# Row transposes into the convolution's bank, both halves of the moments in one run with the transposes of h

## The reference

```python
    h = _L0_tok_ref(x, wte, w1, b1, w2, b2)        # tanh(shifted rows @ w1 + b1) @ w2 + b2
    h = h + _L0_attn_ref(_layernorm(h, axis=-1))   # rfft, |f|^2, top 6 lags, weighted sum
    h = h + _L0_ffn_ref(_layernorm(h, axis=-1), W, bias, A, Bf, coeffs, scales)
    # ffn: x W^T + bias + sum over 16 experts of low rank 16
```

## Time and profile before

| | |
|---|---|
| median of 3 runs | 415.15 us (414.15 to 416.32) |
| the profiled execution | 416.69 us |
| its span, first to last instruction | 414.8 us |
| matrix engine busy | 387.3 us, 93% |
| VectorE, ScalarE, GpSimd busy | 278.6, 246.2, 213.8 us |
| TensorE's granted clock, mean | 0.98 of full speed |
| HBM read, written | 12.40 MB, 67.12 MB |

### The profile page before, as it was taken

One profiled execution on the slowest core, in us unless ns is written; L12 is line 12 of the kernel. 1 busy time (PEld: TensorE's weight loads), 2 busy tenths in 40 slices (PEclk: granted clock), 3 DMA queues, 4 the chain that ended last, 5 costly groups with the idle time before them and its releaser, 6 DMA issues.

```text
span 414.8 us, 6528 instructions
## 1 busy us (share of the span) xinstructions
PE 387.3 (93%) x1908; PEld 280.9 (68%) x1908; DVE 278.6 (67%) x602; ACT 246.2 (59%) x362; POOL 213.8 (52%) x283
## 2 busy tenths in 40 slices
PE   1959987999999999999999999999999999999792
PEld 1535355777777777777777777777777777777461
DVE  3442443968686777777777868586968677776742
ACT  3033335767676767666757576666767676765641
POOL 6772430756647474747373747566555745222200
PEclk9978996999999999999999999999999999999998
DMA  8953010555454555555454555655546555555565
GB/s 191 370 200 111 0 22 2 205 196 232 149 230 174 210 219 212 218 212 212 174 219 164 220 200 205 221 205 182 233 147 233 185 208 218 202 202 202 205 280 230
DMA packets 27684, 79.86 MB, mean 193 GB/s; under 512 B 6186, under 2 KB 7482, under 8 KB 27668
## 3 DMA queue, kind: packets, MB, share of 16 engines
q1 hardware_dynamic: 23330, 75.45, 47.4%
q0 software_dynamic: 4096, 4.20, 4.7%
q10 hardware_dynamic: 242, 0.01, 0.0%
HBM read 12.40 MB, written 67.12 MB: 192 GB/s over the span
## 4 chain that ended last, share of the span: by engine, by line
PE 87%; DMA 3%; DVE 3%; SPq 2%; ACT 2%; issue 1%; ACTq 0%; DVEq 0%
PE o_ps L1057 45%; PE conv_ps L1148 14%; PE conv_ps L1154 7%; PE o_ps L1083 7%; DMA obuf<-in_scales 3%; PE o_ps L990 3%; PE sum_ps L1122 2%; PE mix_ps L1134 2%; PE sum_ps L1134 2%; PE et_ps L1112 2%; PE sum_ps L1096 1%; PE et_ps L1102 1%; SPq L313 1%; PE o_ps L1034 1%; DVE u_lo L868 1%
## 5 line engine op out<-in xcount | busy, mean ns | idle before, releaser
L405 POOL DMA_INDIRECT gathered<-in_wte,idx_now x128 | 128.2, 1002 | 44.2 <-issue 34.4
L509 ACT ACTIVATE obuf<-o_ps,mean_sb,a_sb 128x512 f32<-128x512 f32 x128 | 99.7, 779 | 80.4 <-PE o_ps L1083 53.0
L693 DVE TENSOR_SCALAR obuf<-o_ps,a_sb,mean_sb 128x512 f32<-128x512 f32 x128 | 102.3, 809 | 55.9 <-PE o_ps L1057 30.1
L1057 PE MATMUL o_ps<-w_hi,u_hi 128*128 128x512 f32 x256 | 111.1, 434 | 5.7 <-DVE u_lo L868 3.9
L1057 PE MATMUL o_ps<-w_hi,u_lo 128*128 128x512 f32 x256 | 101.6, 397 | 0.0
L1057 PE MATMUL o_ps<-w_lo,u_hi 128*128 128x512 f32 x256 | 101.6, 397 | 0.0
L1148 PE MATMUL conv_ps<-et_hl,shift_hi 128*128 128x512 f32 x256 | 66.6, 403 | 5.6 <-DVE et_hl L762 4.9
L1057 PEld LDWEIGHTS o_ps<-w_hi,u_hi 128*128 128x128 f32 x256 | 48.3, 189 | 28.2 <-issue 19.3
L1148 PEld LDWEIGHTS conv_ps<-et_hl,shift_hi 128*128 128x128 f32 x256 | 49.0, 193 | 18.5 <-issue 5.7
L433 POOL TENSOR_SCALAR var_eps<-var 128x8 f32<-128x8 f32 x16 | 3.5, 220 | 111.9 <-DVE var L820 111.9
L1057 PEld LDWEIGHTS o_ps<-w_lo,u_hi 128*128 128x128 f32 x256 | 48.3, 189 | 11.7
(11 more groups left out here) (133 smaller groups left out, 446.7 us busy)
## 6 DMA issues: line engine op xcount, KB each, us to landing
out<-obuf SPq DMA_DIRECT2D x63, 1024.0 KB, 4.0
h_all<-in_wT SPq DMA_DIRECT2D x4, 1024.0 KB, 12.6
gathered<-in_wte,idx_now POOLq DMA_INDIRECT x128
aT_sb<-in_aT SPq DMA_DIRECT2D x1, 1024.0 KB, 9.4
bfT_sb<-in_bfT SPq DMA_DIRECT2D x1, 1024.0 KB, 15.5
obuf<-in_w SPq DMA_DIRECT2D x2, 256.0 KB, 5.4
lagged<-xbar_twice SPq DMA_DIRECT2D x1, 512.0 KB, 3.7
out<-obuf SPq DMA_DIRECT2D x1, 512.0 KB, 3.9
```

The source lines that it names most:

```text
L405: pool.indirect_dma_start(gathered[p][:, i, :], None, wte, bass.IndirectOffsetOnAxis(ap=idx_now[p][:, i:i + 1].bitcast(U32), axis=0),).the ...
L509: nc.scalar.activation(obuf[:, q, i % 2, 0:512], o_ps[:, 2 * (i % 2), :], ACT.Identity, bias=mean_sb[pc][:, i:i + 1], scale=a_sb[pc][:, i: ...
L693: nc.vector.tensor_scalar(obuf[:, q, i % 2, 512:L], o_ps[:, 2 * (i % 2) + 1, :], a_sb[pc][:, i:i + 1], mean_sb[pc][:, i:i + 1], ALU.mult, ...
L1057: last = mm(o_ps[:, 2 * (i % 2) + n, :], lhsT, rhs[:, 512 * n:512 * (n + 1)], start=(i % 2 == 0 and f == 0), stop=(i % 2 == 1 and f == len ...
```

## The change

The row transposes write `conv_ps` in place of `et_ps`, and ScalarE (L519) and VectorE (L762) read them there. They now wait for `shifts_added` of the sequence before (the last reader of `conv_ps`), and in step 0 for `pad_conv_kept`, which `conv_half(0)` waited for until now. The second half of the moments is written to `et_ps` in place of `sum_ps` and stands directly behind the first half, ahead of the row transposes and odd tile 0; it waits for `xt_kept` of the sequence before in place of `h_ready`. `transpose_scaled` no longer waits for `et_lo_kept` ahead of the x transposes. No instruction with operands is added or removed.

```diff
@@ -192,7 +192,7 @@
         def y_view(hh):
-            return (mix_ps, sum_ps)[hh][:, 0:4 * (E + 3)].rearrange("p (j two n) -> p j two n", j=2, two=2)
+            return (mix_ps, et_ps)[hh][:, 0:4 * (E + 3)].rearrange("p (j two n) -> p j two n", j=2, two=2)
@@ -517,7 +517,7 @@
                         nc.scalar.copy(tiles_of(et_hl[u][0:E, PAD:SPAN], odd_tiles),
-                                       pair_bank(et_ps, odd_tiles)).then_inc(et_hi_kept, 1)
+                                       pair_bank(conv_ps, odd_tiles)).then_inc(et_hi_kept, 1)
@@ -759,7 +759,7 @@
-                        nc.vector.tensor_tensor(lo, pair_bank(et_ps, odd_tiles), hi.bitcast(F32), ALU.subtract).then_inc(et_lo_kept, 1)
+                        nc.vector.tensor_tensor(lo, pair_bank(conv_ps, odd_tiles), hi.bitcast(F32), ALU.subtract).then_inc(et_lo_kept, 1)
@@ -1097,7 +1097,6 @@
                     pe.wait_ge(x_ready, b + 1)
-                    ge(pe, et_lo_kept, 2 * (a + front))
                     for q in range(NT // 2):
@@ -1106,10 +1105,11 @@
                 def transpose_rows():
                     pe.wait_ge(rows_gathered[u], 16 * NT * (g + 1))
-                    ge(pe, et_lo_kept, 2 * a)
-                    ge(pe, xt_kept, a - 1)
+                    if in_step(0, g, u):
+                        pe.wait_ge(pad_conv_kept, 1)
+                    ge(pe, shifts_added, 2 * a)
                     for j in range(NT // 2):
-                        last = tr(et_ps[:, P * j:P * (j + 1)],
+                        last = tr(conv_ps[:, P * j:P * (j + 1)],
@@ -1127,8 +1127,8 @@
                     if hh == 1:
-                        pe.wait_ge(h_ready, b + 1)
-                    bank, width = (mix_ps, sum_ps)[hh], 2 * (E + 3)
+                        ge(pe, xt_kept, b)
+                    bank, width = (mix_ps, et_ps)[hh], 2 * (E + 3)
@@ -1139,7 +1139,6 @@
                     if in_step(0, g, u) and hh == 0:
                         pe.wait_ge(shift_set, 2)
                         pe.wait_ge(pads_set, 2)
-                        pe.wait_ge(pad_conv_kept, 1)
@@ -1187,12 +1186,11 @@
                 if mid:
                     transpose_h()
                     moments_of(0)
+                    moments_of(1)
                 if front:
                     transpose_rows()
                 if back:
                     odd_tile(0)
-                if mid:
-                    moments_of(1)
                 if back:
                     even_tile(1)
                     four_rank_terms(1)
```

## The result

| | before | after |
|---|---|---|
| median | 414.65 us (413.12 to 416.32, 4 runs) | 421.27 us (420.91 to 422.13, 4 runs) |
| ratio | | 1.0167, 95% interval 1.0132 to 1.0203 |
| the profiled execution | 416.69 us | 421.24 us |
| its span | 414.8 us | 419.3 us |
| matrix engine busy | 387.3 us, 93% | 388.4 us, 93% |

What follows compares the result with a forecast made beforehand. The matrix engine, carrying 87% of the chain that ended last, was taken to bound the kernel. Terms 0 + 5.2 + 1.6 = 6.8 us on the median 415.15 gave 422.0 us, range 419.5 to 424.5.

Steps and rivals of the forecast that it cites:

- the matrix engine's own work: Steps 2 to 16: the four moved fp32 records take 0.46 us in either place, so joining the groups gains 0.
- stall of the convolution, 14 steps: At the first half of the convolution, waiting for VectorE's L762: 0.37 us in each of 14 steps, 5.2 us.
- the first step: Row transposes wait for pad_conv_kept until 25.58, the convolution comes 1.98 us later or more; +1.6 us taken, clock open.
- the end: Step 16 has the move but no convolution, and was given 0.
- The step on which I decided: Odd tile and VectorE's unbroken chain to L762 move 0.46 us later; the convolution has 0.09 room and stalls 0.37.
- Rival (c): Convolution not held by VectorE, the 0.05 us being its load's start anyway; only the first step left, 416.7 us; chance 0.05.
- Rival (a): At the convolution, the weight load overtakes the long wait: stall 0.26 us, 3.6 in 14 steps, total 420.4; chance 0.05.
- the sum by the row: At the convolution, against the skill's rule: the load itself starts 0.05 us after VectorE's end, 14 times of 14.
- the cheap case: First step: the slow clock stretch moves with the idle time, 0.85 us is won back, and the term is +1.1.
- the case that costs the same: First step: the slow clock stretch costs the same as before, and the term is +2.0 us.
- (d): First main product behind each fp32 group: joining saves 0.09 us in 15 places, 1.3 us; total 413.3; chance 0.03.
- (e): Stall in each step, or the longer first-step one, brings another slow clock stretch, 2.5 us or more: 424.5 and above; chance 0.06.

Runs made afterwards that it cites:

- the wait covered: Changed kernel with ScalarE's padding copy early and VectorE's low parts (L762) ahead of the second half of the variance: 413.27 us against 414.13, ratio 0.9988.
- the half move: Kernel before, with only one of the two products of the moments' second half ahead of the row transposes: 418.55 us against 413.62, ratio 1.0084.
- the second profile of the changed kernel: The changed kernel itself, unaltered, measured once more against the kernel before: 420.76 us against 413.62, ratio 1.0160.
- the banks alone: Changed kernel with the moments' second half back behind the first odd tile, new banks kept: 416.10 us against 414.13, ratio 1.0054.
- three pairs of kernels: Joined kernels with waits covered, against unjoined: 413.27 against before's 414.13; 408.28 against 409.34 (bias copy late in both); 406.96 against 407.62 (small loads early in both).
- VectorE's order alone: Kernel before, with only VectorE's low parts put ahead of the second half of the variance: one execution, 418.08 us against 414.02.
- the first four experiments: Moments moved alone on the kernel before (419.68 us); on the changed kernel: moments moved back (416.10), padding copy early (419.03), that plus low parts early (413.27).
- the first experiment: Kernel before, with only the moments' second half moved up, into conv_ps, rows staying in et_ps: 419.68 us against 414.13, ratio 1.0146.

## Why the prediction was right, point by point

The forecast was 422.0 us in 419.5 to 424.5, made as 415.15 + 6.8. Measured are 421.27 us, and +6.6 against the median of before in the same comparison (+7.1 in the second). By its terms:

| term | forecast | measured |
|---|---|---|
| the matrix engine's own work | 0 | step with the wait covered 21.90 against 21.91 |
| stall of the convolution, 14 steps | 5.2 | 14 x 0.365 = 5.1; alone +5.6 by the medians, 4.4 to 7.7 by the ratio, +5.0 group by group (last section) |
| the first step | 1.6 (1.1 to 2.0) | 2.0 by the medians, 1.3 to 3.1 by the ratio |
| the end | 0 | -0.3 |
| sum | 6.8 | 6.8 by these terms; 6.6 and 7.1 by the medians |

**The stall.** The step on which I decided holds in all its parts. The odd tile ends 0.46 later against the even tile ahead of it (VectorE's idle time before it grows from 0.46 to 0.92), VectorE's chain moves with it, the load follows L762 by 0.05, and 0.09 of it is absorbed: half the delay gave a step of 22.05, which is 0.14 above 21.91. Rival (c), that the 0.05 was an accident, would have left the step at 21.91 in the half move and in the whole one. Rival (a), by which the weights are loaded ahead of the wait, falls at the same place: the load starts at 209.91, behind the wait, and is idle for 0.54 before it. The Trainium skill ("TensorE: Matmul & The Clock Gate", What happens when you issue a matmul) says that weight loads are pulled ahead of matmuls in flight. Here the wait stands ahead of both the load and its matmul, and the load was not pulled ahead of it in any of the 14 steps; the sum by the row was right.

**The first step.** The wait was named rightly, and the price of the move as well: the transposes start at 25.58, as worked out. The uncertain part was the clock. In the profile after, the slow stretch is 21.98 to 28.81 instead of 26.37 to 33.20:

```profile
21.98:28.81 6.83, 3.23 (x10) 2.29 (x11) 1.43 (x3) 3.14 (x5) 2.91 (x5) 0.50 0.59 207
```

Only 3.2 us of work lie in it, where it was 5.6. So in this execution the stretch moved with the idle time, as in the cheap case, and the delay at the convolution of step 1 is 0.9 (54.89 against 53.95). In the second profile of the changed kernel the stretch is 2.2 us later, and the same convolution starts at 55.94, 2.0 behind before, as in the case that costs the same.

One step further on this delay is gone from both profiles. In step 1 the matrix engine stands still for 3.0 us, in the kernel before too, and the slow stretch behind that differs in length from execution to execution (stretches of the kernel before and after, then the step-2 convolution of each):

```profile
63.92:70.74 6.82, 6.04 (x22) 4.60 (x23) 1.71 (x4) 2.27 (x4) 0.00 (x0) 0.50 0.01 2
...
66.35:69.77 3.42, 3.42 (x14) 2.16 (x14) 0.81 (x1) 0.80 (x2) 0.00 (x0) 0.50 0.00 0
...
76.11 2.02 PE L1148 MATMUL conv_ps<-et_hl,shift_hi 128*128 128x512 f32 x8
...
76.09 2.13 PE L1147 MATMUL conv_ps<-et_hl,shift_hi 128*128 128x512 f32 x8
```

The second profile of the changed kernel has no slow stretch there, and its step-2 convolution starts at 75.65. So the two profiled executions differ by 4.55 us (421.24 against 416.69), near 5.1 for the loop's stalls less 0.3 at the end: the first step adds nothing to it. The prediction had named 423.5 us for the profiled execution. The first step's price rests on the times alone, 2.0 by the median of the banks alone (by the mean too), with an interval from 1.3 to 3.1. The working knew nothing of the second stretch, which alone moves a run by more than this whole term. That the forecast's 1.6 comes so near the measured 2.0, and the sum with it so near 6.8, is therefore in part luck; what it priced rightly is the delay as far as step 1, 0.9 and 2.0 in the two profiles against 1.1 and 2.0 in its two cases.

**What the sum missed.** The end gets shorter by 0.3 us. From the slot of the step-15 convolution to the end are 53.7 us before and with the banks alone, and 53.4 in every kernel with the whole move. In step 16 of the kernel before, VectorE's last step of u_lo meets GpSimd's copy of h (VectorE and GpSimd, kernel before):

```profile
386.24 1.00 DVE L845 TENSOR_TENSOR u_lo<-hT 64x512 fp32r<-64x512 f32 x1
...
385.97 0.73 POOL L449 COPY h_all<-u_rows 128x512 f32<-128x512 f32 x1
```

and after:

```profile
391.09 0.69 DVE L845 TENSOR_TENSOR u_lo<-hT 64x512 fp32r<-64x512 f32 x1
...
391.30 0.95 POOL L449 COPY h_all<-u_rows 128x512 f32<-128x512 f32 x1
```

With the variance later, VectorE's instruction comes first and runs at its usual 0.69; the matrix engine's wait behind it falls from 1.88 to 1.56. The two go together in all eleven profiles that have no slow stretch there: 1.00 and 53.7 in the four without the move, 0.69 and 53.4 in the seven with it. No run changes this order by itself.

**The rivals' other claims.** (d), that joining the fp32 products saves 0.09 in 15 places: with every new wait covered, three pairs of kernels give the joined one 0.9, 1.1 and 0.7 us less, none of them clear of noise. The profiles account for about 0.5: 0.3 at the end, and 0.015 per step, half of which VectorE's order gives alone. The pairs also differ in VectorE's order and in the banks. The profiles do not show the 1.3 us, and the times alone don't exclude them. (e), that an idle time of some tenths brings down the clock: from step 3 to 15 the changed kernel keeps the full clock with a stall in each step. But behind the idle time near 386 a slow stretch does follow in two profiles (the half move, VectorE's order alone), which I had excluded because none did in the profile of before.

## What to carry to other kernels

Work that is moved past an evacuation moves that evacuation and all that the other engine does behind it, even where the moving engine's own sum is zero; look for the consumer whose load starts the same few hundredths behind a release in every step, for there the room is already used up. When a wait is moved to an earlier instruction, count everything that stands between the two in the same queue, and ask what stands ahead of the signal on the signalling engine: here a copy of 0.14 us stood behind a 13 us wait for two small transfers that it did not need. Reorder the waiting engine's work before giving such a change up: moving two lines on VectorE covered the stall.

## What the runs showed that I had not expected

The runs of one kernel fall into groups according to where the slow stretches of the clock lie. Of the 21 runs of the kernel before beside the first four experiments, 10 took 412.7 to 413.6 us, 7 took 414.1 to 415.1 and 4 took 415.9 to 416.6. Of the first experiment's six, three took 418.0 to 418.3 and three 421.0 to 421.5, nothing between; its profile is of a 418.1 run, and there the stretch behind the second step's idle time is missing (60 to 75 at the full clock):

```profile
60.00:75.00 15.00, 11.86 (x62) 8.56 (x61) 9.06 (x19) 9.95 (x15) 2.81 (x6) 1.00 0.18 70
```

The step-2 convolution stands at 73.3 there and at 76.1 in the kernel before, whose profile is slow from 63.92 to 70.74 and is otherwise the same up to that point within 0.5 us. One such stretch costs some 2.7 us, an estimate from this pair: 76.1 - 73.3, less the 0.5 by which the one was ahead already, and with the 0.4 of its stall in step 2. So a first step whose idle time is changed by 2 us can show +0.9 or +2.0 at step 1 of a single profile and nothing at step 2, and only many runs give its price. Set lowest group against lowest and highest against highest (a grouping made after the fact), the run of fp32 products alone costs 5.0 and 4.9 us, closer to the profiles' 5.1 - 0.3 than the 5.6 of the medians. In the same way the kernel with the stall covered lies 0.6 and 0.4 below before, near the 0.5 that the profiles account for and not at the 1.3 of rival (d).

GpSimd and VectorE slow each other where both read the scratchpad: L845, both inputs in SBUF, takes 1.00 us beside GpSimd's copy and 0.69 alone, and the copy 0.95 where it comes second, 0.73 where it comes first, and 0.60 to 0.63 where neither holds up the other. The Trainium skill, "SBUF — State Buffer", Who interferes with whom, says that a VectorE instruction with two SBUF inputs contends with a GpSimd one that reads SBUF, and that the order of issue decides who waits; the trace agrees with both.
